# A vision tower on one core: keys and queries share one set of matmul products, and the embedding's normalised rows are made by two fused VectorE steps

## The reference

```
p  = 196 patches of 16x16x3                      # 196 x 768
h  = LN(p)*g + b;  h = h @ W + b;  h = LN(h)*ln2_g + ln2_b   # 196 x 192, "h1"
a  = LN(h)                                       # no gain
q, k, v = split(a @ w_attn + b_attn);  q *= 1/4  # 12 heads of 16
s  = q k^T + q rel^T, causal;  y = softmax(s) v
h2 = h + y @ w_proj + b_proj
z  = LN(LN(h2))*g1 + b1 ...                      # routing: 29 of 196 tokens get a second
                                                 # attention, the others a mix of rows
h3 = ... ;  out = h2 + h3 + gelu(LN(h3)*g2+b2 @ W1 + bf1) @ W2 + bf2
```

## Time and profile before

| | |
|---|---|
| median of 3 runs | 5028.85 us |
| profiled execution, own time | 5031.06 us |
| its span, first to last instruction | 5029.3 us |
| TensorE busy | 4843.7 us (96%), granted clock 0.988 of full |
| VectorE busy | 3993.2 us (79%) |
| ScalarE busy | 3540.8 us (70%) |
| GpSimd busy | 3230.6 us (64%) |
| DMA | 302 MB, 60 GB/s |

### The profile page before, as it was taken

How to read it: one execution, slowest core, us unless ns; L and a number is a source line. 1 busy time by engine, 2 the same in 40 slices (tenths; PEclk the granted TensorE clock), 3 DMA queues, 4 the chain that set the end, 5 groups by cost and what they waited for, 6 DMA issues and landing times. The chain is left out here.

```text
span 5029.3 us, 146877 instructions
## 1 busy us (share of the span) xinstructions
PE 4843.7 (96%) x46680; PEld 4523.8 (90%) x46680; DVE 3993.2 (79%) x12888; ACT 3540.8 (70%) x12158; POOL 3230.6 (64%) x4399
## 2 busy tenths in 40 slices
PE   3999999999999999999999999999999999999998
PEld 2899999999999999999999999999999999999997
DVE  3788888888888888888888888888888888888885
ACT  0677777776777777777777677777777777777775
POOL 2566666666666666666666666666666666666664
PEclk6999999999999999999999999999999999999999
DMA  5444444444444445444444444444444444444440
GB/s 68 56 65 62 55 64 61 59 62 61 61 59 64 61 55 67 62 55 65 61 59 62 61 61 59 64 61 56 67 62 55 65 61 59 62 61 61 59 64 16
DMA packets 338231, 302.00 MB, mean 60 GB/s; under 512 B 46796, under 2 KB 305177, under 8 KB 338201
## 3 DMA queue, kind: packets, MB, share of 16 engines
q1 hardware_dynamic: 325950, 298.98, 43.3%
q10 hardware_dynamic: 12251, 2.65, 0.4%
HBM read 205.18 MB, written 19.27 MB: 45 GB/s over the span
## 5 line engine op out<-in xcount | busy, mean ns | idle before, releaser
L1615 ACT ACTIVATE p<-banks,negmax 98x98 f32<-98x98 f32 (+1 forms) x3072 | 1138.9, 379 | 184.8 <-DVE negmax L1237 121.3
L539 POOL TENSOR_TENSOR p<-p,rden 98x392 f32<-98x392 f32 x1152 | 953.6, 842 | 384.0 <-DVE rden L1253 379.5
L1237 DVE TENSOR_REDUCE negmax<-banks 98x2 f32<-98x392 f32 (+1 forms) x1152 | 626.2, 553 | 51.4 <-PE banks L743 51.2
L743 PE MATMUL banks<-kz,qk_parts 128*98 128x392 f32 x2304 | 632.8, 385 | 0.0
L778 PE MATMUL banks<-ident,p 98*98 98x98 f32 x4608 | 550.7, 251 | 69.9 <-ACTq L1619 64.4
L1615 ACT ACTIVATION_READ_ACCUMULATOR p<-banks,negmax 98x1 f32 x3072 | 610.3, 199 | 0.0
L754 PE MATMUL banks<-tokw,x_sb 128*98 128x193 f32 x3072 | 572.7, 336 | 15.5 <-POOLq L551 15.5
L530 POOL TENSOR_TENSOR gparts<-gT,gparts 128x392 fp32r<-128x392 f32 x384 | 398.3, 1050 | 270.8 <-DVE gparts L1433 270.8
L754 PEld LDWEIGHTS banks<-tokw,x_sb 128*98 128x98 f32 x3072 | 541.7, 252 | 18.0 <-issue 15.5
L778 PEld LDWEIGHTS banks<-ident,p 98*98 98x98 f32 x4608 | 415.8, 129 | 140.0 <-ACTq L1619 90.8
L695 PE MATMUL banks<-z3Ts,w_split 128*128 128x196 f32 x3840 | 534.7, 286 | 4.8 <-DVE z3Ts L1211 3.9
(11 more groups left out here) (273 smaller groups left out, 12470.1 us busy)
## 6 DMA issues: line engine op xcount, KB each, us to landing
x_sb<-in_x SPq DMA_DIRECT2D x384, 196.0 KB, 5.0
kz<-gparts SPq DMA_DIRECT2D x512, 147.0 KB, 2.9
x_sb<-in_x SPq DMA_DIRECT2D x256, 190.8 KB, 8.8
x_sb<-in_x SPq DMA_DIRECT2D x256, 185.5 KB, 10.9
x_sb<-in_x SPq DMA_DIRECT2D x128, 189.0 KB, 7.3
out<-out_row SPq DMA_DIRECT2D x128, 147.0 KB
pT<-in_L_ffn_W ACTq DMA_DIRECT2D x1, 576.0 KB
gstore<-in_L_ffn_W SPq DMA_DIRECT2D x1, 384.0 KB
```

What stands on the lines that cost most here:

```text
L539: gp.tensor_tensor(heads, heads, rden[:, g, t, s0:s0 + sn].unsqueeze(2).broadcast_to([HT, sn, w]), ALU.mult).then_inc(sem["pnorm_sb"], 1)
L743: last = mm(o, qparts[:, g, HT * t:HT * t + HT], kz[:, part, slots[0]:slots[-1] + 1, g, 0:w], start=False, stop=part == 1, skip_group_chec ...
L1237: ve.tensor_reduce(negmax[:, g, t, slots[0]:slots[-1] + 1], bank[RING[f"S{k}"]][0:HT, 0:w * len(slots)].rearrange("p (s w) -> p s w", w=w) ...
L1615: sc.activation((p1 if t else p0)[0:HT, 4 * g + s], bank[b][0:HT, w * i:w * i + w], ACT.Exp, bias=negmax[:, g, t, s:s + 1], accum_out=den[ ...
```

## The change

**One set of products.** The weights of keys and queries are laid out together: for each group of four heads, 64 columns of keys (one row per head dimension, no doubling) and 64 columns of queries. One call `keys()` makes both for image l; the bias and the relative rows come in by one sixth product.

```diff
-            def group_cols(b0, w, name):
-                for g in range(NG):
-                    ... five products, and one of add_parts or bqparts
...
+                def keys():
+                    if front:
+                        pe.wait_ge(sem["pT_act"], after("pT_act", n, evacuation("A4")[1]))
+                    else:
+                        pe.wait_ge(one["w_ready"], 1)
+                    pe.wait_ge(sem["aTs_sb"], after("aTs_sb", l))
+                    for g in range(NG):
+                        o, at = grouped(2)[:, g], slice(128 * g, 128 * g + 128)
+                        for i, (p, wpart) in enumerate(PAIRS):
+                            mm(o, split["wkq"][:, wpart, at], aT[:, p], start=i == 0, stop=False)
+                        last = mm(o, add_w[:, at], rel_ones[:], start=False, stop=True)
+                    last.then_inc(sem["kq_mm"], 1)
```

ScalarE and VectorE split that result once (`kqhi_sb`, `kqlo_sb`; 128x588 each), and `query_parts` and ScalarE's `queries` are gone. SP places it with ten DMAs instead of four:

```diff
             def place_keys(n):
-                sp.wait_ge(sem["klo_sb"], after("klo_sb", n))
+                sp.wait_ge(sem["kqlo_sb"], after("kqlo_sb", n))
                 for s in range(4):
-                    at = slice(32 * s, 32 * s + 32)
-                    sp.dma_start(kz[at, :, s].bitcast(F32),
-                                 kparts[at].bitcast(F32)).then_inc(sem["kz_in"], 16)
+                    for r in range(2):
+                        at = 64 * r + DH * s
+                        sp.dma_start(kz[at:at + DH, s].bitcast(F32),
+                                     kq[DH * s:DH * s + DH].bitcast(F32)).then_inc(
+                                         sem["kz_in"], 16)
+                for part in range(2):
+                    sp.dma_start(qparts[64 * part:64 * part + 64].bitcast(F32),
+                                 kq[64:128, part].bitcast(F32)).then_inc(sem["q_in"], 16)
...
             with sp.Fori(0, B - 4) as j:
-                place_keys(j + 2)
                 prefetch(j + 3, j + 4)
+                place_keys(j + 3)
                 store(j)
```

```diff
+                def embedding_scaled():
+                    ve.drain()
+                    for t in range(2):
+                        ve.scalar_tensor_tensor(y_row[:, t], y_row[:, t], mv_y[:, t, 0:1], ln2g[:],
+                                                ALU.subtract, ALU.mult)
+                    ve.drain()
+
                 def embedding_normalised():
                     ve.wait_ge(sem["y_rstd"], after("y_rstd", l))
-                    normalise(y_row, y_row, mv_y, rstd2, "y_norm")
+                    if front:
+                        ve.wait_ge(sem["h1b_sb"], after("h1b_sb", n))
+                    for t in range(2):
+                        last = ve.scalar_tensor_tensor(h1[:, t], y_row[:, t], rstd2[:, t:t + 1],
+                                                       ln2b[:], ALU.mult, ALU.add)
+                    last.then_inc(sem["h1_sb"], 1)
```

More of the change, by code:

```diff
@@ L198, in build @@
         pT1 = sb("pT1", [128, NH, HT])
-        yhi, yparts = qhi, qparts
+        yhi = sb("yhi", [128, NG, T], F32R)
+        yparts = sb("yparts", [128, NG, T], F32R)
         h2 = sb("h2", [HT, 2, D])
@@ L363, in build @@
             for p in (0,) if chunk == 0 else (0, 64):
[L364 to L368, removed]
+                for j, at in enumerate((D, 0)):
+                    load(halves(raw["wkq"][p:p + size, chunk])[:, j],
+                         wa[lo:hi, at:at + D].rearrange("p (g w) -> p g w", g=NG))
                 load(raw["wv"][p:p + size, chunk], wa[lo:hi, 2 * D:3 * D])
@@ L990, in attention_cols @@
                     pe.wait_ge(sem["a_sb"], after("a_sb", l))
-                    rows_to_cols(1, a_row, "aT_mm")
-                if front:
-                    keys()
+                    if front:
+                        pe.wait_ge(sem["pT_act"], after("pT_act", n, evacuation("B1")[1]))
+                    rows_to_cols(2, a_row, "aT_mm")
                 if back:
@@ L1481, in step @@
                     kept_rows()
-                    q_blocks()
                 if front:
-                    maxima(4)
+                    inverse_sums(0)
                     inverse_sums(1)
@@ L1489, in step @@
                     inverse_sums(2)
+                    maxima(4)
                     maxima(5)
+                    inverse_sums(3)
                     maxima(6)
-                    inverse_sums(3)
+                if back:
+                    q_blocks()
+                if head:
+                    patch_variance()
+                if front:
                     inverse_sums(4)
                     maxima(7)
-                    inverse_sums(5)
                 if back:
                     max2()
-                if tail:
-                    mlp_cols_lo()
                 if front:
-                    inverse_sums(6)
-                    transposed("A0")
+                    inverse_sums(5)
                 if head:
-                    patch_variance()
+                    embedding()
                 if back:
```

337 lines of the change are left out of this document (155 added, 182 removed).

## The result

The kernel after takes 4948.21 us (median of 4 runs, 4944.02 to 4953.14), the one before 5029.01 in the same comparison: a ratio of 0.984 (95%: 0.9823 to 0.9857), 81 us or 1.6% faster. The forecast was 4831. Sign and range held; the gain is less than half of the 198 us forecast.

A forecast was written before the change was run, and what follows sets the result against it. TensorE was taken as the bound: 37.34 us of work less 2.14, plus waits of 0.15, 0.7 and 0.4, gives 36.45 a step; 128 x 1.53 plus 2 is 198 us saved, 4831 us. Range 4675 to 4970.

The forecast's parts named there:

- Where the new order waits: TensorE's new waits in a step: 0.15 behind z0's transposes, 0.7 by up(2), 0.4 at projection.
- Wait ahead of keys2, 0.15: After z0's transposes, ScalarE's and VectorE's halves take 1.35 us, TensorE covers 1.24: wait about 0.15 us.
- VectorE and TensorE at max2 together: After scores2, VectorE and TensorE both arrive at 16.7 us from routed_cols; max2 takes 0.7, to 17.5.
- ScalarE's stretch to gelu 1 of 7.95: From softmax2 to gelu 1's end ScalarE is the chain: 7.95 us instead of 10.3, ending at 25.5.
- Projection 0.4: At projection, yparts come late because only scatter covers VectorE's parts: wait 0.4 us, bounds 0.2 and 1.0.
- The embedding's rows: Two fused pairs on VectorE, 0.92 us each; VectorE's work stays about 32.7 us; POOL's lost operations only give slack.
- Placement without a wait: Ten placement DMAs land 5.5 to 6.9 us after routed_cols, before S0 at 7.0: no wait, upper bound 2.0.
- Set-up and filling: Before and around the full steps: 4 us gained in set-up (bounds 0 and 15), about 2 lost in filling.
- 1 (no waits): TensorE stays the only bound, the three waits absent: 35.2 to 35.4 us a step, 4685 us; chance 0.24.
- 3 (placement late): Placement lands late and S0 waits 2.0 us: 38.45 us a step, 5090 us; chance 0.11.
- Rival 4: VectorE's or ScalarE's queue takes all the gain: 37.9 us a step, 5025 us; chance 0.04.
- Rival 2: Fused steps and POOL's operations hold each other, two waits of 0.84 us: 37.45 a step, 4960 us; chance 0.13.

The follow-up runs named there:

- experiment 1: Kernel after with all 18 products of keys made twice: 5200.8 us, a step of 39.38 against 37.40.
- the third buffer: Kernel after with a third buffer for the Gelu's output and gelu 2 ahead of the attention columns' copy: 4948.66 us.
- experiment 5, second kernel: Kernel before with only the fused row pairs added, embedding_scaled placed behind A3 and inverse_sums 8: 5025.13 us, ratio 0.9993.
- experiment 6: Kernel after with keys ahead of scatter and projection, values ahead of routed_cols: 5469.59 us, ratio 1.0872.
- experiment 5 with the rows as before: Kernel after with the fused rows undone, VectorE normalising and POOL multiplying and adding again: 5311.87 us, ratio 1.0561.

## Why the prediction was wrong

**The step that failed is the sum of waits in "Where the new order waits": 1.25 us forecast, 37.40 - 35.20 = 2.20 measured, 0.95 too little, 128 x 0.95 = 122 us of error.** The mechanism was right in kind: TensorE's work shrinks and the new order opens waits. Their size was wrong, and of the two branches behind softmax 8 it followed only ScalarE's. Where they lie is read by comparing each stretch of TensorE's calls, start to start, with the same calls in the old step without its two waits (us; all from the two timelines of the earlier trace rows and above):

| stretch | after | same calls before | more | forecast |
|---|---|---|---|---|
| routed_cols to S0 | 7.33 | 6.87 | 0.46 | 0.15 |
| S0 to transposes2 | 13.94 | 13.73 | 0.21 | 0.7 with the next |
| transposes2 to up(2) | 4.98 | 4.17 | 0.81 | |
| up(2) to keys | 5.91 | 5.15 | 0.76 | 0.4 |
| keys and down | 5.24 | 5.28 | -0.04 | 0 |
| sum | 37.40 | 35.20 | 2.20 | 1.25 |

So every one of the three terms was too small, by 0.31, 0.32 and 0.36. The two waits that the forecast had a reason for came out near their size: 0.81 against 0.7 ahead of up(2), and, from scatter to projection, 0.83 us against 0.36, so 0.47 against 0.4. What was missing is 0.35 instead of 0.15 behind mlp_cols (0.64 us to keys2 where the same transposes took 0.29), and gaps of about 0.1 us at calls to which the forecast gave none: keys2, mixing_rows, scores2, attn_out, attention_cols, projection. By the forecast's own milestones, counted from routed_cols (forecast, measured): S0 7.0, 7.33; softmax2 17.5, 18.22; up(2) 25.5, 26.25; end 36.45, 37.40. So it slipped 0.33 up to S0, 0.39 between S0 and softmax2, 0.03 from there to up(2), and 0.20 behind it.

Point by point:
- TensorE bound: right in sense. Ten products added cost their full 1.10 us at keys; but only 0.77 at up(0), where other engines' chains are 0.33 us from taking over.
- 2.14 us less of products: right; they measure 1.98 (experiment 1). TensorE's instructions 44376 against 44380.
- Wait ahead of keys2, 0.15: 0.35. The two halves behind the transposes were put at 1.35 us; VectorE's ends at 2505.44, 1.55 after 2503.89, where values follows the transposes. The profile books the wait at the weight load (49.4 us over the span), nearly none at the products (7.5).
- VectorE and TensorE at max2 together, softmax2 at 17.5: late by 0.72, of which 0.33 is S0's. They do arrive together (max2 waits 0.26 us for scores2), but ScalarE, which I had not counted there, is the engine without a gap between S0 and softmax2; behind a softmax it often stands 0.16 us with nothing that the profile shows to wait for (121.8 us over the span in 744 places). Which of the three sets this stretch was not isolated.
- ScalarE's stretch to gelu 1 of 7.95: 7.98 (2521.82 to 2529.80), right, and not the bound it was taken for: without the table load the step keeps its length. Branch B, which the forecast counted only by VectorE's total (32.7, "fits"), is nearly as long.
- Projection 0.4: 0.47 by the calls' starts, of which the profile books 0.23 at the products; it follows attention's end, and gelu 2 is no part of it (the third buffer).
- The embedding's rows: wrong in three ways. They cost 0.75 + 1.32 us, not 2 x 0.92. The 0.92 was itself a held pair, and the earlier trace rows had been misread (last section). And POOL's two operations gone are no mere slack: in this order they would stop VectorE 1.79 us, and the step would be 2.8 us longer. POOL's busy time fell by 165 us, not 257, and VectorE's by 3.0%, not under 1%: POOL's normalising grew (a mean of 870 ns, where the median stays at 842), and VectorE's rows beside POOL shrank (last section).
- Placement without a wait: right, narrowly. The last landing, forecast for 5.5 to 6.9 after routed_cols, comes at 6.8 to 7.2; an S0 at the forecast 7.0 would have been within 0.2 us of waiting.
- Set-up and filling: 2 gained forecast; outside the steps, counted as 128 like the forecast's, 9 measured. VectorE's wait for the last weight ends 8.6 us earlier, at 46.88 against 55.51, where 4 had been assumed; the first output row is only 4.9 us earlier, so filling lost some 4, not 2:
```profile
46.88 0.46 DVE L1085 COPY pT<-bv 128x294 f32<-128x294 f32 x1 [20.73 <-DMA pT<-in_L_ffn_W]
```
- Rivals: 1 (no waits) and 3 (placement late) are excluded; 4 (nothing) too. Rival 2 (the fused steps and POOL hold each other, 37.45 a step, 4960 us) gave nearly the measured number, but for a reason that is only half its own: the holding is there (next section), yet halving the held operation alone brought nothing. It counts only together with branch A, and one hold of 0.6 us a step is shown, not two of 0.84. That its 4960 lies within 12 us of the measured time is luck for the most part.
- The bounds: the sum of 0.2 to 3.0 us of waits does not give 4690 to 4950. With 3.0 the step is 38.20 and the time about 5060; 4950 is what 2.2 us of waits give. Rival 4's 37.9 a step is 5017 rather than 5025. The range held with its stated top, 22 us above the measurement.
- None of the three signs named against the forecast appeared (S0 waiting over 0.3, VectorE idle under 2, no wait at up(2) and projection): they would have shown other mechanisms, not waits of twice the size.

What stays open: whether a kernel that does all the work can shorten both branches; the one that leaves work out shows 0.6 us a step in them. The table says where TensorE's excess lies; what each of its small gaps waits for was not taken apart (groups such as the 16 transposes at 2527.74, 2.11 us where the same took 1.72, stretch by waits too short to be listed), nor which engine sets the 13.94 us from S0 on.

## What to carry to other kernels

Work taken from the bounding engine is gained only where its queue has no second engine's chain of nearly the same length beside it: before forecasting, write down every chain that ends within the amount to be removed, for all engines, with the short gaps between dependent instructions in it, not only totals. Where shortening one suspect changes nothing, shorten two together; a gain that appears only then shows parallel branches. And a change of order can turn a harmless hand-over into a stop: price the moved instruction by what stands behind it in its queue, which cost 1.1 us a step in one place and nothing two calls later. A last one on reading: where a median and a maximum stand far apart, look at single instructions; half of them may be at the maximum.

## What the runs showed of the hardware

- VectorE operations with two SBUF inputs and POOL's hold each other. The fused pair L1273 takes 0.75 us; the pair L1282, which meets POOL's normalising, takes 1.32, one operation about 0.41 and the other about 1.00. The durations over the span (ns min/median/max), VectorE's and POOL's:
```profile
L1282 DVE SCALAR_TENSOR_TENSOR h<-y_row,rstd,ln2b x256: 407/556/998, 92.4 to 4845.6; 98x192 f32<-98x192 f32 x128
```
```profile
L544 POOL TENSOR_TENSOR p<-p,rden x1152: 839/842/1401, 117.4 to 4883.4; 98x392 f32<-98x392 f32 x192
```
  In the kernel before with the fused rows placed later (experiment 5, second kernel) the two pairs change parts. The first pair runs beside POOL's normalising (2533.70 to 2534.54) and is held, the second runs with POOL idle and is not:
```profile
2533.71 1.37 DVE L1280 SCALAR_TENSOR_TENSOR y_row<-y_row,mv_y,ln2g 98x192 f32<-98x192 f32 x2
2535.22 0.75 DVE L1289 SCALAR_TENSOR_TENSOR h<-y_row,rstd,ln2b 98x192 f32<-98x192 f32 x2
```
  The earlier trace rows had 403/416/591, which the forecast took as no holding. That median hid two groups of equal size. The first operation of the pair at 2522.04, beside POOL's product, takes 0.59 us and ends 0.2 after it (2522.41); the second takes 0.41:
```profile
2522.04 0.59 DVE L1335 SCALAR_TENSOR_TENSOR f<-mrow,keep,f 98x192 f32<-98x192 f32 x1
```
- The placement's DMAs, from SBUF to SBUF, hardly follow their size: 73.5 KB land in 2.6 us (median) and take 0.62 each to issue, 147 KB in 2.7 to 2.9 and 0.62 to 0.63.
- The granted clock fell behind TensorE's waits. In experiment 6, after the waits of 1.25 and 1.07 us shown there, a stretch had 0.75 of full clock, so about half of it at the lower of the two levels, 1.2 GHz, and the ten products of keys2 took 1.65 us from their start to the next call's, where the kernel after has 1.10:
```profile
2517.85:2524.70 6.85, 6.85 (x47) 6.72 (x48) 2.96 (x15) 3.90 (x8) 2.86 (x4) 0.75 0.07 23
```
  So part of that kernel's 4 us a step is the clock's. Over its span it has 0.943, the kernel after 0.989. The kernel of experiment 5 with the rows as before shows the same behind its wait of 1.62 us.
